# Queries and keys turned as 80 columns a chunk and copied into place by on-chip transfers, in an attention and mixture-of-experts kernel

## The reference

```python
q, k = rms_norm(q), rms_norm(k)
q = apply_rotary_emb(q, cos, sin); k = apply_rotary_emb(k, cos, sin)
q = q * q_gain
scores = einsum('bqhgd,bkhd->bhgqk', qg, k) * scale      # causal, softmax
y = einsum('bhgqk,bkhd->bqhgd', attn, v)
x = x + ternary_linear(rms_norm(y), w_proj)              # weights rounded to -1, 0, 1 times a scale
x = x + experts(layernorm(x)) + shared(layernorm(x))     # 8 experts, the best 2 of each token
```

## Time and profile before

| | us |
|---|---|
| median of three runs (range) | 596.61 (595.45 to 596.68) |
| the profiled execution's own time | 590.83 |
| its span, first to last instruction | 589.0 |
| PE, ACT, DVE, POOL busy | 490.4, 364.2, 340.9, 166.8 |
| mean granted PE clock, of full speed | 0.92 |

### The profile page before, as it was taken

The page is one execution under the profiler, slowest core; times in us unless marked ns, Lnnn a source line. Parts: engine busy times, 40 slices in busy tenths (PEclk is TensorE's granted clock), DMA queues, the critical chain, the costliest instruction groups (busy, mean ns, idle before and its releaser), DMA issues.

```text
span 589.0 us, 10118 instructions
## 1 busy us (share of the span) xinstructions
PE 490.4 (83%) x3328; PEld 276.6 (47%) x3328; DVE 340.9 (58%) x972; ACT 364.2 (62%) x567; POOL 166.8 (28%) x221
## 2 busy tenths in 40 slices
PE   1586889997999999999989888939697979999930
PEld 1583323233333333333334333417585869998920
DVE  6975566843581235812246766364967757666626
ACT  4253778883899878998777867535452335555520
POOL 4501101011101021010242227125455834444430
PEclk9887989897999999999999999779799899999975
DMA  8999999000000000000132003122011333444349
GB/s 230 299 304 306 279 7 2 2 1 1 1 1 1 1 2 1 1 0 1 37 99 86 26 1 114 45 85 73 15 60 48 94 101 101 125 124 120 110 139 344
DMA packets 66390, 49.84 MB, mean 85 GB/s; under 512 B 24552, under 2 KB 64072, under 8 KB 66344
## 3 DMA queue, kind: packets, MB, share of 16 engines
q1 hardware_dynamic: 62936, 39.89, 30.1%
q0 software_dynamic: 3408, 9.34, 4.4%
HBM read 19.88 MB, written 29.34 MB: 84 GB/s over the span
## 4 chain that ended last, share of the span: by engine, by line
PE 58%; DVE 16%; issue 11%; ACT 4%; POOL 4%; DMA 4%; SPq 1%; ACTq 0%; POOLq 0%; DVEq 0%
PE ps L1479 18%; PE ps L1459 12%; PE ps L1662 6%; PE ps L1443 5%; PE ps L1680 3%; ACT prob L696 3%; PE ps L1608 2%; PE ps L1488 2%; PE ps L1409 2%; DVE qk L973 2%; PE ps L1684 2%; POOL rows_by_expert L580 1%; PE ps L1671 1%; DMA yfin<-pair_out 1%; PE ps L1653 1%
## 5 line engine op out<-in xcount | busy, mean ns | idle before, releaser
L696 ACT ACTIVATE prob<-ps 128x1024 f32<-128x1024 f32 (+3 forms) x320 | 262.3, 916 | 85.3 <-PE ps L1459 84.3
L1479 PE MATMUL ps<-prob,v_sb 128*32 128x512 f32 (+3 forms) x1280 | 157.9, 567 | 12.2 <-POOL prob L539 8.5
L1459 PE MATMUL ps<-qk 50*128 50x512 f32 (+3 forms) x640 | 120.4, 441 | 8.9 <-ACT prob L696 5.6
L539 POOL TENSOR_SCALAR_AFFINE_SELECT prob<-prob 128x512 f32<-128x512 f32 x64 | 41.2, 645 | 253.4 <-ACT prob L696 253.2
L1459 PEld LDWEIGHTS ps<-qk 50*128 50x128 f32 x640 | 53.7, 193 | 92.8 <-ACT prob L696 69.1
L973 DVE CAST qk<-ps 128x512 fp32r<-128x512 f32 (+1 forms) x48 | 33.1, 691 | 68.7 <-PE ps L1443 68.7
L1479 PEld LDWEIGHTS ps<-prob,v_sb 128*32 128x32 f32 x1280 | 25.8, 110 | 57.6 <-issue 28.7
L641 POOL DMA_INDIRECT pair_out<-yo,xg x39 | 37.4, 959 | 54.3 <-DVE yo L1345 54.0
L1443 PE MATMUL ps<-ident,stack 128*128 128x128 f32 x192 | 33.0, 297 | 10.5 <-DVE qk L973 8.5
L1443 PEld LDWEIGHTS ps<-ident,stack 128*128 128x128 f32 x192 | 21.2, 146 | 42.6 <-issue 41.7
L1608 PE MATMUL ps<-x2T,ws_hi 128*128 128x512 f32 (+1 forms) x96 | 32.4, 420 | 5.1 <-DVE hid L1214 5.1
(11 more groups left out here) (205 smaller groups left out, 802.7 us busy)
## 6 DMA issues: line engine op xcount, KB each, us to landing
rows_by_expert<-pads SPq DMA_DIRECT2D x9, 1935.0 KB, 20.6
xg<-rows_by_expert SPq DMA_DIRECT2D x39, 129.0 KB, 2.2
yfin<-pair_out SPq DMA_DIRECT2D x8, 512.0 KB, 7.0
stage<-in_w SPq DMA_DIRECT2D x8, 352.0 KB
x_sb<-in_x SPq DMA_DIRECT2D x4, 512.0 KB, 6.2
res<-in_x SPq DMA_DIRECT2D x4, 512.0 KB, 4.0
out<-y_sb SPq DMA_DIRECT2D x4, 512.0 KB, 5.2
stage<-in_w SPq DMA_DIRECT2D x8, 176.0 KB
```

Source lines behind the costliest of these rows:

```text
L539: nc.gpsimd.affine_select(out=t, in_=t, compare_op=ALU.is_ge, fill=0.0, base=0, pattern=[[0, HPG], [1, P]], channel_multiplier=-1).then_in ...
L696: nc.scalar.activation(prob[:, u % NPB, 2 * hf:2 * hf + 2, c0:CH], ps[:, b:b + 2, c0:CH], ACT.Exp, scale=SCALE).then_inc(exp_done, 1)
L1459: ins = M(ps[:, 2 * (n % NSB) + h, c0:CH], qk[rows, par, PAIRS, kt * P:(kt + 1) * P], qk[rows, par, hf, j * CH + c0:(j + 1) * CH], start=T ...
L1479: ins = M(ps[VW * h:VW * (h + 1), O_BANK, c0:CH], v_sb[:, kt, :], prob[:, u % NPB, h, c0:CH], start=(kt == 0), stop=(u == LAST_OF[j]), ski ...
```

## The change

`stack` and `split` are gone. A round is now a chunk: PE turns the 80 rotated columns of `wk_b` (four query heads, one key head) of four tiles into rows 0 to 79 of the bank, DVE takes a high part and a low part of these rows to a new buffer `qT`, and SP copies 16-row pieces of `qT` to their places in `qk` by DMA: 12 for the queries and 6 for the keys of a chunk, and with chunk 0 four more for the shift rows. The shift is turned once, in the prologue; the ones are set by POOL. The first scores that need a chunk wait on `ld_qk[j]`. The transfers of group g and the clearing share SP's queue in the order shown. `ternary` uses `wk_c` as its scratch instead of `wk_b`.

```diff
-RPC = 3
-ROUNDS = RPC * NC
+ROUNDS = NC
...
+QK_MOVES = [3 * HPG + 6 + (HPG if c == 0 else 0) for c in range(NC)]
...
-NEXT_ROUNDS = {26 + r: [("round", 1, r)] for r in range(ROUNDS - 2)}
-NEXT_ROUNDS[NU - 1] = [("round", 1, r) for r in (ROUNDS - 2, ROUNDS - 1)]
+NEXT_ROUNDS = {28 + 2 * r: [("round", 1, r)] for r in range(ROUNDS)}
 FIRST_GROUP = {
...
+    0: [("round", 0, 1)], 4: [("out", 0, 0)], 8: [("round", 0, 2)], 12: [("out", 0, 1)], 16: [("round", 0, 3)],
+    24: [("out", 0, 2)], **{30 + 2 * r: [("round", 1, r)] for r in range(ROUNDS)}, NU - 1: [("weights",)],
 }
...
+            sp.wait_ge(ones_ready, 2)
+            sp.wait_ge(shift_ready, 1)
...
+            def move(g, c):
+
+                sp.wait_ge(x_free, round_use(g, c))
+                par, cs = (g + 1) % 2, slice(c * CH, (c + 1) * CH)
+                for hf in range(2):
+                    for h in range(2):
+                        head, at = 2 * hf + h, SLOT * h
+                        for part, n in ((0, 0), (1, 1), (0, 2)):
+                            sp.dma_start(qk_f[at + n * HD:at + (n + 1) * HD, par, hf, cs],
+                                         qT_f[head * HD:(head + 1) * HD, part, cs]).then_inc(ld_qk[c], 16)
+                for h in range(2):
+                    for part, n in ((0, 0), (0, 1), (1, 2)):
+                        at = SLOT * h + n * HD
+                        sp.dma_start(qk_f[at:at + HD, par, PAIRS, cs], qT_f[HPG * HD:QKD, part, cs]).then_inc(ld_qk[c], 16)
...
+            for c in range(NC):
+                move(0, c)
             sp.wait_ge(consts, CONSTS)
...
+            clear_rows(0, 3)
+            for c in range(NC):
+                move(1, c)
+            sp.wait_ge(s_ready, 2 * NU)
+            clear_rows(3, blocks)
+            for c in range(NC):
+                move(2, c)
+            sp.wait_ge(zeroed, 16 * blocks)
...
+            for c in range(NC):
+                move(3, c)
 
             sp.wait_ge(s_ready, 2 * NU * (NKV - 1))
             sp.dma_start(res[:], x_t[:, 0:TPC, :]).then_inc(ld_res, 16)
 
             sp.wait_ge(x_free, X_LAST)
+            for c in range(NC):
+                sp.wait_ge(ld_qk[c], 16 * QK_MOVES[c] * NKV)
...
+            for par in range(2):
+                nc.gpsimd.memset(qk[:, par, PAIRS, :].bitcast(F32), 1.0).then_inc(ones_ready, 1)
...
+            def take_round(g, c):
+
+                next_use()
+                if not (isinstance(g, int) and g == 0):
+                    dve.wait_ge(ld_qk[c], 16 * QK_MOVES[c] * g)
+                hi, lo = (qT[0:QKD, part, c * CH:(c + 1) * CH] for part in range(2))
+                link(V.tensor_copy(hi, ps[0:QKD, X_BANK, :]))
+                V.tensor_tensor(lo, ps[0:QKD, X_BANK, :], hi.bitcast(F32), ALU.subtract).then_inc(x_free, 1)
...
+            dve.wait_ge(shift_psum, 1)
+            V.tensor_copy(shT[:], ps[0:2 * NH, X_BANK, 0:P]).then_inc(shift_ready, 1)
             dve.wait_ge(qkv_ready, TPC)
             norm_qk(0, 0, TPC)
+            rotate(0, TPC)
             low_part_x(1)
+            take_round(0, 0)
             low_part_x(2)
-            round_weights(1, D // P)
-            rotate(0, TPC)
-            dve.wait_ge(small_done, SMALL_STEPS)
-            split(0, 0, TPC)
-            low_part_x(3)
             dve.wait_ge(qkv_ready, 2 * TPC)
             norm_qk(0, TPC, 2 * TPC)
-            take_rounds(1, 0, RPC)
+            low_part_x(3)
+            round_weights(1, D // P)
+            rotate(TPC, 2 * TPC)
             dve.wait_ge(qkv_ready, NT)
             values(0)
             for c in range(1, NC):
...
+                take_round(0, c)
                 if c < NC - 1:
+                    norm_qk(0, TPC * (c + 1), TPC * (c + 2))
+                    output(0, c - 1)
                     rotate(TPC * (c + 1), TPC * (c + 2))
...
             turn_x(1)
...
+            turn_x(2)
+            turn_round(0, 1)
+            project(1)
+            turn_x(3)
+            project(2)
+            project(3)
...
+                    if hf == 0 and kt == 0:
+                        pe.wait_ge(ld_qk[j], 16 * QK_MOVES[j] * (g + 1))
```

More of the change, by code:

```diff
@@ L66 @@
 RES_AFTER = {4: 1, 7: 2, 8: 3}
-CONSTS = 25
+CONSTS = 23
 NXG = 8
-NEXT_ROUNDS = {26 + r: [("round", 1, r)] for r in range(ROUNDS - 2)}
-NEXT_ROUNDS[NU - 1] = [("round", 1, r) for r in (ROUNDS - 2, ROUNDS - 1)]
+NEXT_ROUNDS = {28 + 2 * r: [("round", 1, r)] for r in range(ROUNDS)}
 FIRST_GROUP = {
[L76 to L80, removed]
+    0: [("round", 0, 1)], 4: [("out", 0, 0)], 8: [("round", 0, 2)], 12: [("out", 0, 1)], 16: [("round", 0, 3)],
+    24: [("out", 0, 2)], **{30 + 2 * r: [("round", 1, r)] for r in range(ROUNDS)}, NU - 1: [("weights",)],
 }
@@ L99, in uses, with round_use @@
     return sum(len(v) for v in schedule.values())
-X_FIRST = RPC
+X_FIRST = 1
 X_MID = X_FIRST + uses(FIRST_GROUP)
 X_LAST = X_MID + (NKV - 2) * uses(MID_GROUP)
+def round_use(g, c):
+    if g == 0 and c == 0:
+        return 1
+    schedule, base = (FIRST_GROUP, X_FIRST) if g < 2 else (MID_GROUP, X_MID + (g - 2) * uses(MID_GROUP))
+    before = [v for u in sorted(schedule) for v in schedule[u]]
+    return base + before.index(("round", min(g, 1), c)) + 1
 ORDER = [v for u in sorted(LAST_GROUP) for v in LAST_GROUP[u]] + [v for u in sorted(AFTER) for v in AFTER[u]]
@@ L238, in build @@
         shift_parts = sb("shift_parts", [P, NH, 2], F32, prep)
+        shT = sb("shT", [2 * NH, P], F32R, prep)
         wqT = sb("wqT", [P, KD, QKV], F32R, prep)
@@ L285, in build @@
         qkv_ready = sem("qkv_ready")
-        stack_ready = sem("stack_ready")
+        rot_ready = sem("rot_ready")
+        shift_psum = sem("shift_psum")
+        shift_ready = sem("shift_ready")
+        ones_ready = sem("ones_ready")
+        ld_qk = [sem(f"ld_qk{c}") for c in range(NC)]
         x_full = sem("x_full")
@@ new lines, in clear_rows @@
+            def clear_rows(b0, b1):
+                for b in range(b0, b1):
+                    sp.dma_start(rows_d[b * PADS * P:(b + 1) * PADS * P, :].rearrange("(k p) c -> p k c", p=P),
+                                 pads[:].broadcast_to([P, PADS, ROW])).then_inc(zeroed, 16)
+            blocks = ROWS // (PADS * P)
+            for c in range(NC):
+                move(0, c)
+            sp.wait_ge(consts, CONSTS)
+            clear_rows(0, 3)
+            for c in range(NC):
+                move(1, c)
@@ L407, in _ @@
+            sp.wait_ge(s_ready, 2 * NU)
[3 more added lines that the diff above has]
+            sp.wait_ge(zeroed, 16 * blocks)
+            for b in range(blocks):
                 sp.dma_start(rows_d[b * PADS * P:(b + 1) * PADS * P, ID:ID + 1].rearrange("(k p) c -> p k c", p=P),
@@ L937, in rotate @@
                 link(V.tensor_tensor(flat(b), flat(a), flat(c), ALU.add))
[L939 to L958, removed]
+                dve.sem_inc(rot_ready, 1)
             xuse = {"base": 0, "n": 0}
@@ L1034, in _ @@
             rotate(0, NT)
-            split(1, 0, NT)
             group_scales(1, D // P)
             ternary(1, D // P)
-            take_rounds(0, 0, ROUNDS - 4)
+            for c in range(NC):
+                take_round(1, c)
             copy_output(0, NC - 1)
@@ L1054, in _ @@
                 rotate(0, NT)
-                split(g + 1, 0, NT)
                 output(g, 2)
-                take_rounds(g % 2, 0, ROUNDS - 2)
+                for c in range(NC):
+                    take_round(g + 1, c)
                 copy_output(g, NC - 1)
                 values(g + 1)
-                take_rounds(g % 2, ROUNDS - 2, ROUNDS)
                 assert xuse["n"] == uses(MID_GROUP)
@@ L1566, in attend @@
                     if u < NU:
-                        if isinstance(g, int) and g == 0 and UNITS[u][1] == 0 and UNITS[u][0] > 0:
-                            pe.wait_ge(x_free, xuse["base"] + xuse["n"])
                         scores(g, u, (g + 1) % 2)
                     elif following:
-                        if u == NU:
-                            pe.wait_ge(x_free, xuse["base"] + xuse["first chunk"])
                         scores(g + 1, u - NU, g % 2)
@@ L1577, in attend @@
                     exchange(g, schedule, q, parts_next)
-            for r in range(RPC):
-                turn_round(r, 1)
-            pe.wait_ge(x_free, RPC)
             for u in range(LAG):
```

85 lines of the change are left out of this document (32 added, 53 removed).

## The result

Four runs of the changed kernel have a median of 672.8 us (670.5 to 674.6), four of the kernel before on the same chip 596.0: a ratio of 1.129 (interval 1.124 to 1.134), slower. Some executions of a kernel are a per cent slower than its others with no change to it; the ratios leave these out, the medians don't. The forecast had the sign and 607.3. The profiled execution took 674.6, its span was 672.6 against 589.0, so 83.6 of difference have to be found in the two traces; the medians differ by 76.8. On the page, the chain of work that ended last had SP's queue at 1%.

A forecast was written before the change was run, and what follows sets the result against it. Attention was taken as bound by PE where a round stands, by ACT elsewhere. +4.7 through group 1's start, -5.1 and -5.7 for groups 1 and 2, +14.9 and +1.9 for group 3: +10.7 on 596.6, 607.3 us; whole range 593 to 622.

The forecast's parts named there:

- the size of an issue: SP's queue: each 16-row move issues in 0.42 us (bounds 0.34 and 0.51), 7.6 for 18, 32 for 76.
- POOL's two new memsets: Prologue: they lie in POOL's idle time before the small loads land and cost nothing.
- Group 2: Its chunk 0, turned in group 1, needs 12.8 us and has 17; clearings end at about 210, before being in the way.
- Group 3's term: Weight pieces issue behind all 76 moves, so PE's values product of unit 4 stands 14.9 us later than it would.
- The removed rounds: Groups 1 and 2: twelve rounds a group become four, gaining 5.1 us in group 1 and 5.7 in group 2.
- positions 26 to 35: Groups 1 and 2: ten rounds, 22.4 us, become 19.2 with four rounds, a gain of 3.2.
- position 39: Two rounds in a row took 2.4 us there; without them, less 0.5 for waits, a gain of 1.9.
- The lower clock: PE returns slower after long idle: +1.5 us for one spell in group 0, +1.9 after group 3's wait.
- the issue is short: Rival: 16 rows might issue in 0.1 us, so moves hardly queue; -24, 573 us, faster; chance 0.16.
- The transfers themselves are slow: Rival: rows between few partitions need more than an issue, say 0.6 us each; 31 more, 638 us; chance 0.08.

The follow-up runs named there:

- e1: Computation left out; SP only issues runs of 12 transfers: 0.63 us each from SBUF to SBUF, 0.45 for 16 rows with HBM on one side.
- e10: As e1, other forms: SBUF to SBUF with 16 rows of 6 KB 0.82 us, HBM to HBM 0.62, POOL issuing 0.49 each.
- e4: Changed kernel, chunks 1 to 3 moved together from group 1 on, 40 issues a group in place of 76: 652.9 us, ratio 1.092.
- e7: Changed kernel, ACT issuing nine of the 18 moves for each of chunks 1 to 3 of group 0: 653.1 us, ratio 1.106.
- e2: Changed kernel with POOL's two fills of ones behind its small steps in place of ahead of them: 668.0 us, ratio 1.119.
- e5: Kernel before with only POOL's two fills of ones added, DVE waiting for them ahead of its first round: 596.1 us, ratio 1.008.
- e6: Changed kernel, three of the six clearing transfers between group 1's and group 2's moves put behind group 2's moves: 673.4 us, ratio 1.137.
- e3: Changed kernel, in group 3 DVE copies chunk 0's output before taking the first two weight pieces: 671.3 us, ratio 1.125.
- e9: Kernel of e8 with the four rounds of the next group three positions sooner in every group: 624.5 us, ratio 1.051.
- e11: Kernel of e9 with POOL in place of ACT as second issuer, in every group: 617.8 us, ratio 1.031.
- e8: Changed kernel with the edits of e2, e4 and e7 together: 631.7 us, ratio 1.068.

## Why the prediction was wrong in size

**The step that failed is the size of an issue**, "so I take 0.42 (bounds 0.34 and 0.51)". It measured 0.63 from one issue to the next, alone on the chip [e1, e10] and in the changed kernel, outside the bounds. The rows that I extrapolated were of transfers between HBM and SBUF, and I carried on along rows and pieces. The number of rows hardly moves the price of one issue (0.42 and 0.43 at 16 and 128). What moves it is where both ends lie, and no row of the kernel before had both in SBUF. Why the ends matter no run shows. About 0.03 of the missing 0.21 is another slip: the rows give the duration of one issue, and from one to the next it is that much more (0.42 and 0.45 between HBM and SBUF, 0.59 and 0.63 from SBUF to SBUF). Put into the forecast's own sum, 0.21 more for each is: three chunks of 18 in group 0, 11.3; chunk 0 in the prologue, 33.4 + 22 x 0.63 + 2 = 49.3 in place of 46, so 3.3; 40 issues at group 1, 8.4; 76 ahead of group 3, 16.0. That is 39 us: 646. e4 and e7 show that it is the number of issues that counts: fewer issues for the same bytes gave 20 us, the same issues on two engines 14.

**That POOL's two new memsets cost "nothing" failed.** They cost 3.4 us of the prologue and, over whole runs, about 5 [e2, e5]. That they lay in POOL's idle time was right; what they stopped was DVE.

**Group 2 was taken as covered, and wasn't.** The clearings were to end at about 210; at SP's queue they ended at 234.5, because the moves before them ended late and six of them took 30 us. Chunk 0's first twelve moves then took 14.0 where 7.5 is their price. That is the 10.7 us of idle, of which 7.9 went with the clearings [e6]. Without them 2.8 remain: the round, DVE, 22 issues and the landing need from 230.1 to 249.4, 19.2 us, and have 16.4, where the forecast had 12.8 with 17 to cover them. Three steps of the forecast are in this one wait: the price of an issue, the order in SP's queue, and a cover that held only at 0.42. Group 2 was forecast at -5.1 and came at +12.2, group 3 at -5.7 and came at +3.5.

**Group 3's term had the right mechanism.** SP issued the pieces behind all 76 moves, DVE stood by them for 27.6 us and PE for 25.6. The forecast's 14.9 plus 16.0 for the issues would be 31; 26.8 was measured. e3 shows that the stall would have come whatever DVE did first, and e4 that it goes with the queue.

**The removed rounds gave what was computed in one place of two.** From the first scores behind group 2's last own output turn to its end (262.53 to 289.10 before, 310.24 to 333.43 now, where the wait begins) it is 3.4 us less, where the forecast had 3.2 for positions 26 to 35. The 1.9 of position 39 did not come, which the next point shows.

**The lower clock was counted too small** (3.4 us in all). The mean granted clock fell from 0.920 to 0.836. PE's busy time for scores and values products, the same 1920 matmuls, rose from 278.3 to 303.0 us, and all but some 3 of that lies before unit 4's values product of group 3. Units 0 to 3 of group 2 show it best. The windows (from:to, us, then busy time and instructions of PE, PEld, DVE, ACT, POOL, granted clock, DMA share, GB/s) are, before and after:

```profile
215.30:223.28 7.98, 6.79 (x66) 3.16 (x62) 2.22 (x4) 5.09 (x8) 3.01 (x5) 1.00 0.01 2
```

```profile
257.04:268.24 11.20, 9.51 (x52) 3.55 (x53) 1.77 (x7) 5.10 (x8) 2.55 (x4) 0.50 0.21 52
```

Of the 3.2 us more, 1.4 are the wait for unit 4. The rest, 1.8, stands against a forecast of -1.9: two rounds are gone, but PE came from a wait of 10.7 us and ran the whole stretch at 0.50, the 1.2 GHz level. Group 3's stretch in the table, -5.7 forecast and +3.5 measured, comes apart in this way, from the two timelines: 3.7 for the waits in front of its units 0 and 4, 3.0 for the lower clock behind unit 4 of group 2 (268.24 to 280.11, for 223.28 to 232.14), 2.3 for units 0 to 3 (the forecast's 1.9, and 0.4 more), which is 9.0 of 9.2.

**The last stretch, +8.3, is not the price of the wait in front of it.** From unit 4's values product of group 3 on, the two kernels do the same work. At equal places the distance is 1.2 us soon behind the wait, where PE comes back at a granted clock of 0.50 (1.94 us for 1.06), and stays so for 58 us. Then 4.2 more come at once. The chain of work that ended last has this there, and ACT's timeline the same wait:

```profile
435.50 4.15 another core or an unknown queue
```

```profile
439.67 0.59 ACT L766 CAST x2T<-ps 128x512 fp32r<-128x512 f32 x1 [4.17 <-remote]
```

ACT's cast waits for something that the trace doesn't name, and a second one does at 488.69, for 3.13 us. The other runs set this apart from the wait in front. Counted from the same values product to the end, the kernel before needed 286.6 us and e5 286.1. e7, which waited 25.3 us in front, needed 286.3; e4, which waited 1.1, needed 296.7. In all runs with waits of this kind on ACT, 7.6 to 9.1 us in sum (the changed kernel, e2, e4, e9, e11), it is 292.9 to 296.7; in those with none (before, e5, e6, e7, e8) 286.1 to 290.6. e3 has another order there. What ACT waits for is open, and so is why only some of the kernels have it.

The sum: 607.3 + 39 for the issues + 4.8 for the fills + 8 for the clearings is 659. The remaining 14 us were not taken apart by a run. The traces show enough to fill them, the last stretch, the short waits of groups 2 and 3 and the lower clock, but they are of one execution each, whose difference is 7 us more than that of the medians.

The rivals: *the issue is short* had the sign of the error wrong: the issue is longer than every row of before. *The transfers themselves are slow* had the time nearer (638), which was luck: its 0.6 us a move is close to what was measured, but its cause is not, as 16 rows of 0.5 KB and of 2 KB cost the same. The sentence of the Trainium skill that stood beside the first one (DMA: Bandwidth & Descriptors, Issuing engines are not separate DMA queues), that a second issuing engine saves only the time to initiate, which is usually small, has its other side here: that time was most of the wait, and a second issuer took it from 12.2 to 6.9 us [e7].

## What to carry to other kernels

Before work goes from an engine to the DMA queues, count the issues on the busiest queue between "the source is ready" and "the first reader", and price them by a row whose two ends lie where the new ones lie: 18 copies from SBUF to SBUF are 11 us, whatever their size up to 4 KB a row. Then list what stands behind them in that queue (here: clearings and weight pieces), for it is late by the whole run, and check that what covers them still does at that price. If such copies must be, make them few and wide, share them between issuing engines that wait for nothing else, and put a large fill on POOL where DVE is idle.

## What the runs showed of the hardware that was not expected

- SP's issue in a run of twelve: 0.62 to 0.64 us from SBUF to SBUF with 1 to 128 rows of 2 KB, and with 16 rows of 0.5 and 4 KB; 0.62 from HBM to HBM; 0.45 between HBM and SBUF with 16 rows in either direction, 0.58 from HBM with 128 rows. From SBUF to SBUF with 16 rows of 6 KB it was 0.82, of 8 KB 1.10, and with 128 rows of 6 KB 1.28. One execution each.
- POOL issued moves of 16 rows of 2 KB in 0.49 us each; ACT and SP at once in 0.63 and 0.65.
- A POOL fill of 128x2048 (3.55 us for two) held a DVE cast for 3.3 us in one kernel and a DVE operation on 128x4 elements for 3.1 in another.
